# Attention of a fused perceiver layer: nine of 17 key tiles of the probabilities turned by VectorE and DMAs

## The reference, cut to what matters

```
q      = layernorm(x) @ Wq          # 32 heads of 128, in 4 groups of 8
k, v   = concat(ctx, layernorm(x)) @ Wk, @ Wv    # 2048 + 128 = 2176 keys, 4 KV heads
scores = q k^T / sqrt(128)          # 128 x 2176 per head
attn   = softmax(scores)
x      = x + (attn @ v) @ Wo
```

## Time and profile before

| | us |
|---|---|
| median of three runs | 699.45 (698.38 to 700.05) |
| the profiled execution | 698.99 |
| its span in the trace | 697.3 |
| TensorE busy | 671.9 (96%) |
| VectorE, ScalarE, GpSimd busy | 436.9, 356.7, 117.1 |
| granted TensorE clock, mean | 0.988 of full speed |

### The profile page before, as it was taken

How to read it: one execution, slowest core, us unless ns; L and a number is a source line. 1 busy time by engine, 2 the same in 40 slices (tenths; PEclk the granted TensorE clock), 3 DMA queues, 4 the chain that set the end, 5 groups by cost and what they waited for, 6 DMA issues and landing times.

```text
span 697.3 us, 12695 instructions
## 1 busy us (share of the span) xinstructions
PE 671.9 (96%) x4450; PEld 575.4 (83%) x4450; DVE 436.9 (63%) x1095; ACT 356.7 (51%) x706; POOL 117.1 (17%) x75
## 2 busy tenths in 40 slices
PE   7999998999999999999999987997999999999897
PEld 6888887899999999999999977996797797796453
DVE  2533115767777777677677765779857757756562
ACT  4403116667776677678766652664435435434101
POOL 0000001112431143114321133022220220200100
PEclk9999999999999999999999999998999999999989
DMA  8511001011021110311031503953577667647702
GB/s 257 240 61 60 1 1 61 1 56 67 1 71 52 64 56 0 120 60 60 0 111 50 240 12 145 293 199 144 203 242 264 223 238 274 214 175 276 283 20 98
DMA packets 15701, 87.07 MB, mean 125 GB/s; under 512 B 3584, under 2 KB 3968, under 8 KB 6064
## 3 DMA queue, kind: packets, MB, share of 16 engines
q1 hardware_dynamic: 15088, 85.52, 34.0%
q10 hardware_dynamic: 576, 1.05, 0.5%
HBM read 86.30 MB, written 0.26 MB: 124 GB/s over the span
## 4 chain that ended last, share of the span: by engine, by line
PE 92%; DVE 4%; ACT 2%; DMA 1%; issue 1%; SPq 0%; DVEq 0%; ACTq 0%
PE ps L1284 18%; PE ps L1079 15%; PE ps L1080 15%; PE ps L1081 14%; PE ps L1191 8%; PE ps L1324 8%; PE ps L1148 4%; PE ps L1313 2%; PE ps L1396 2%; PE ps L1431 2%; DMA ring<-wk_dram 1%; PE ps L1295 1%; PE ps L1304 1%; PE ps L1296 1%; DVE acc L922 1%; ACT prob L524 1%
## 5 line engine op out<-in xcount | busy, mean ns | idle before, releaser
L711 DVE TENSOR_TENSOR pt_lo<-ps,pt_hi 128x512 fp32r<-128x512 f32 x144 | 95.1, 661 | 72.0 <-ACT pt_hi L442 71.1
L1284 PEld LDWEIGHTS ps<-norm_t,ring 128*128 128x128 f32 x1152 | 132.6, 193 | 4.8 <-issue 3.9
L1284 PE MATMUL ps<-norm_t,ring 128*128 128x128 f32 x1152 | 133.8, 276 | 0.0
L442 ACT ACTIVATE pt_hi<-ps 128x512 fp32r<-128x512 f32 x144 | 82.2, 571 | 85.0 <-PE ps L1191 84.7
L524 ACT ACTIVATE prob<-prob,neg_max 128x512 f32<-128x512 f32 (+1 forms) x128 | 94.6, 741 | 7.5 <-DVE neg_max L803 7.5
L922 DVE SCALAR_TENSOR_TENSOR acc<-raw,cw,acc 128x127 f32<-128x127 f32 (+2 forms) x240 | 78.5, 402 | 27.9 <-ACT acc L622 27.9
L799 DVE TENSOR_SCALAR_CACHE_REDUCE prob<-ps 128x512 f32<-128x512 f32 (+1 forms) x160 | 92.0, 605 | 2.6 <-PE ps L1081 1.2
L1079 PE MATMUL ps<-pt_hi,v_hi 128*128 128x256 f32 x272 | 88.3, 325 | 0.0
L1191 PE MATMUL ps<-ident,prob 128*128 128x128 f32 x544 | 83.2, 273 | 1.9 <-DVE pt_lo L711 1.3
L1191 PEld LDWEIGHTS ps<-ident,prob 128*128 128x128 f32 x544 | 65.2, 140 | 14.9 <-DVE pt_lo L711 2.2
L1080 PE MATMUL ps<-pt_hi,v_lo 128*128 128x256 f32 x272 | 76.4, 281 | 0.0
(11 more groups left out here) (170 smaller groups left out, 1097.6 us busy)
## 6 DMA issues: line engine op xcount, KB each, us to landing
ring<-w_in_dram SPq DMA_DIRECT2D x36, 1024.0 KB, 4.8
ring<-w_out_dram SPq DMA_DIRECT2D x16, 1024.0 KB, 4.8
ring<-wq_dram SPq DMA_DIRECT2D x8, 1024.0 KB, 5.9
ring<-wo_dram SPq DMA_DIRECT2D x8, 1024.0 KB, 4.8
ring<-w_dram SPq DMA_DIRECT2D x4, 896.0 KB, 6.0
ring<-ctx_t_dram SPq DMA_DIRECT2D x3, 1024.0 KB, 6.8
ring<-w_dram SPq DMA_DIRECT2D x3, 1024.0 KB, 4.7
ring<-wk_dram SPq DMA_DIRECT2D x4, 256.0 KB, 8.2
```

The source lines that it names most:

```text
L442: copy = lambda dst, src: nc.scalar.activation(dst, src, ACT.Copy)
L711: sub = lambda dst, a, hi: nc.vector.tensor_tensor(dst, a, hi, ALU.subtract)
L1284: ins = mm(ps[:, bank, t * T:t * T + T], w[:, t, c, :], norm_t[:, c, :], start=(c == 0), stop=(c == NC - 1))
```

## The change

Pairs 0 to 14 are worked differently. Units 0 to 3 (eight key tiles, "near", 1024 keys) stay as they were. Units 4 to 8 (nine tiles, "far", 1152 keys) are no longer transposed by TensorE: VectorE transposes each head's far part in 32x32 blocks within its partitions (`turn_far`), 16 DMAs a pair carry the blocks to their place (`moves`: from 32 partitions to 32 partitions, 2304 bytes each), ScalarE takes `pt_hi` from there, and GpSimd, not VectorE, computes `pt_lo` of these units (`far_split`). The last pair is all on TensorE as before. `prob` becomes two near buffers and one far buffer.

The first four score chunks of a pair are computed two pairs ahead, in units 6, 7 and 8 (`AHEAD_AT`), the other six in units 0 to 2 (`SCORES_AT`). Queries move from unit 5 to 3, the output product from units 6 and 7 to 4 and 5, the output weights' high part from unit 2 to 0. Exps begin with the far pieces. At the start the second pair's queries stand ahead of the first scores, its first four chunks behind them, and the third pair's queries go into pair 0. On SP the weight loads are put between the moves.

```diff
-EXP_AT = ((), (), ((0, 0),), ((0, 1), (0, 2)), ((0, 3),), ((1, 0), (1, 1)), ((1, 2),), ((1, 3),), ())
-K_AT = {2: {5: (0,), 6: (1,), 7: (2,), 8: (3,)}, 3: {0: (4,)}}
+EXP_AT = ((), ((0, 2), (0, 3)), ((0, 0), (0, 1)), ((1, 2), (1, 3)), ((1, 0),), ((1, 1),), (), (), ())
+PE_UNITS = 4
+NEAR = 4 * PE_UNITS * P // 2
+FAR = KV_LEN - NEAR
+FAR_T = FAR // P
+MOVES = 16
+SCORES_AT = ((4, 5), (6, 7), (8, 9), (), (), (), (), (), ())
+AHEAD_AT = ((), (), (), (), (), (), (0,), (1,), (2, 3))
+K_AT = {2: {2: (0,), 3: (1,), 4: (2,), 5: (3, 4)}}
-W_UNIT = 2
-OUT_UNITS = (6, 7)
-Q_UNIT = 5
+W_UNIT = 0
+OUT_UNITS = (4, 5)
+Q_UNIT = 3
...
@@ SP
+            def moves(m):
+                sp.wait_ge(turned, 2 * m + 2)
+                if m >= 2:
+                    sp.wait_ge(pfl_ok, FAR_UNITS * (m - 1))
+                for i in range(4):
+                    for j in range(4):
+                        sp.dma_start(far_t[m % 2][32 * j:32 * j + 32, i, :, :, :],
+                                     blocks_t[32 * i:32 * i + 32, j, :, :, :]).then_inc(moved, 16)
+            moves(0)
+            load(2, wq[2], 2)
+            for n in range(LAST_PAIR - 1):
+                kv, p = n // PAIRS, n % PAIRS
+                if p == 2:
+                    load(0, wo[2 * kv + 2], 3 + kv)
+                if p == 0 and kv:
+                    load(1, wo[2 * kv + 1], 2 + kv)
+                moves(n + 1)
+                if p == 1 and kv < KVH - 1:
+                    load(3, wq[2 * kv + 3], 2 + kv)
+                if p == 3 and kv < KVH - 2:
+                    load(2, wq[2 * kv + 4], 3 + kv)
...
@@ GpSimd
+            def far_split(n, u):
+                w = 2 if u < 8 else 1
+                pool.wait_ge(pth_ok, UNITS * n + u + 1)
+                sub(unit_of(pt_lo[u % 3], w), far_unit(n % 2, u, w),
+                    unit_of(pt_hi[u % 3], w).bitcast(F32)).then_inc(pfl_ok, 1)
...
+                for u in range(PE_UNITS, UNITS):
+                    if n < LAST_PAIR:
+                        far_split(n, u)
+                    if more and p == 2 and u > PE_UNITS:
+                        k_split(kv + 1, u - PE_UNITS - 1)
+                    if more and p == 3 and u == 6:
+                        v_split(kv + 1, 0)
...
@@ ScalarE
+                if u < PE_UNITS or near_only:
+                    act.wait_ge(t_ps, PE_UNITS * n + u + 1)
...
+                else:
+                    act.wait_ge(moved, 16 * MOVES * (n + 1))
+                    copy(unit_of(pt_hi[u % 3], w), far_unit(b, u, w)).then_inc(pth_ok, 1)
...
@@ VectorE
+            def turn_far(m, h):
+                dve.wait_ge(exp_ok, 2 * NPC * m + (2, 6)[h])
+                if h == 0 and not (isinstance(m, int) and m == 0):
+                    dve.wait_ge(moved, 16 * MOVES * m)
+                nc.vector.transpose(blocks_t[:, :, :, h, :].rearrange("p j t q -> p t j q"),
+                                    far[:, h, :].rearrange("p (t j k) -> p t j k", j=4, k=32)).then_inc(turned, 1)
...
+                    if u in (2, 3) and not (last and p >= 2):
+                        turn_far(n + 1, u - 2)
...
@@ VectorE, start
+            q_split(1, 1, 6)
             for c in range(1, 10):
                 scores_out(0, 0, c)
...
+            turn_far(0, 0)
+            scores_out(1, 1, 0)
+            scores_out(1, 1, 1)
+            turn_far(0, 1)
+            scores_out(1, 1, 2)
+            scores_out(1, 1, 3)
+            pt_split(0, 0)
+            pt_split(0, 1)
```

More of the change, by code:

```diff
@@ L262, in out_chunk, with prob, far_unit, unit_of @@
             return step_chunk(g, 4 + i)
+        def prob(b, h, lo, hi):
+            return near[b][:, h, lo:hi] if lo < NEAR else far[:, h, lo - NEAR:hi - NEAR]
+        def far_unit(b, u, w):
+            at = 2 * (2 * u - 2 * PE_UNITS)
+            return far_t[b][:].rearrange("p i t h q -> p i (t h) q")[:, :, at:at + 2 * w, :]
+        def unit_of(tile, w):
+            return tile[:, 0:w, :].rearrange("p w (h i q) -> p i (w h) q", h=2, i=4)
         block = ctx.enter_context(nc.Block())
@@ L550, in attn_step @@
                     tgt = u + 2
-                    if tgt < UNITS or not (last and turn):
+                    if u == 2 and not (last and turn):
+                        for h, i in EXP_AT[u]:
+                            soft_exp(n + 1, 1 - b, h, i)
+                    if tgt < UNITS:
                         act.wait_ge(pv_ps, 9 * n + u + 1)
-                        pt_split(9 * n + tgt, tgt % UNITS, 4 + (9 * p + tgt) % 2)
+                        pt_split(n, b, tgt, last and turn)
+                    elif not (last and turn):
+                        act.wait_ge(pv_ps, 9 * n + u + 1)
+                        pt_split(n + 1, 1 - b, tgt - UNITS, False)
                     if u == 0 and not first:
@@ L560, in attn_step @@
                         wo_split(kv, p)
-                    if not (last and turn):
+                    if u != 2 and not (last and turn):
                         for h, i in EXP_AT[u]:
                             soft_exp(n + 1, 1 - b, h, i)
-                    if u == Q_UNIT + 1 and not first and not (last and p >= 2):
+                    if u == Q_UNIT + 1 and not (last and p >= 2):
                         q_split(n + 2, b, 6 + (1 - b))
@@ L1209, in attn_step @@
                     tgt = u + 2
[L1210 to L1217, removed]
+                    if tgt < PE_UNITS or (last and turn and tgt < UNITS):
+                        pe.wait_ge(ptl_ok, PE_UNITS * n + tgt - 1)
+                        transposes(n, b, tgt)
+                    elif tgt >= UNITS and not (last and turn):
+                        pe.wait_ge(ptl_ok, PE_UNITS * n + 2 + tgt - UNITS + 1)
+                        transposes(n + 1, 1 - b, tgt - UNITS)
                     if u == 0:
@@ L1222, in attn_step @@
                             pe.wait_ge(ql_ok, n + 2)
[L1223 to L1226, removed]
+                    values(n, b, u, kv if p == 0 else None, last and turn)
+                    if not (last and turn):
+                        for c in SCORES_AT[u]:
+                            if turn and c == 4:
                                 pe.wait_ge(kl_ok, NCHUNK * (kv + 1) + c + 1)
@@ L1242, in _ @@
             queries(0, 0, 0, 7)
+            queries(1, 0, 1, 6)
             pe.wait_ge(k_ev, 17)
@@ L1249, in _ @@
                 scores(0, 0, c)
-            queries(1, 0, 1, 6)
-            pe.wait_ge(ql_ok, 1)
-            queries(2, 0, 2, 7)
             queries_done(1, 1)
-            pe.wait_ge(exp_ok, NPC + 1)
-            transposes(0, 0, 0, 0, 4)
-            transposes(0, 1, 0, 1, 5)
+            pe.wait_ge(ql_ok, 2)
+            for c in range(4):
+                scores(1, 1, c)
+            transposes(0, 0, 0)
+            transposes(0, 0, 1)
             attn_step(0, 0, True, False)
```

106 lines of the change are left out of this document (57 added, 49 removed).

## The result

The changed kernel takes 686.20 us (median of four runs, 685.27 to 687.21), the kernel before 698.96 beside it (four runs): 12.8 us less, ratio 0.9819 [0.9802, 0.9835]. The forecast was 678.0 in a range of 672 to 704. So the sign and the range held, and 8 us of the gain that was forecast did not come. Medians of one kernel differ by up to 1.6 us from one set of runs to the next (the kernel before took 698.96, 699.37, 699.31 and 700.55), and one execution of the variant warm, 1321.84 us, is left out together with its trace. The profiled execution took 687.21 us with a span of 685.5; before it was 698.99 with 697.3, so the two spans differ by 11.8 us, against the 21.4 of the sum.

The account below looks back on a forecast made before the run. TensorE was taken to bound the kernel. Start +1.65, pairs 1 to 13 -25.7, late GpSimd +7.4, pair 14 -1.98 - 2.8: total -21.4 from 698.99, giving 677.6, with 0.46 for the median 678; range 672 to 704 us.

Parts of the forecast that it names:

- rival (a): A part is late (ScalarE copies, GpSimd at 1.5 to 1.8 us, or a common port): still faster, 684 to 698; chance 0.21.
- The bound and the gross gain: In attention, time is what TensorE issues; 18 transposes fewer a pair save 1.98 us, 29.7 us over 15 pairs.
- Durations taken from other rows: Times of new instructions, from nearest profile rows: VectorE turn 1.36 us, GpSimd far subtraction 1.29 and 0.75, ScalarE copy 0.62.
- rival (c): GpSimd's far subtraction in pieces of 32 is slow: gain gone at 1.83 us, total 709 at 2.0; chance 0.09.
- Late GpSimd in third and fourth pairs: GpSimd's K and V splits delay far groups: 1.7 us in third pairs, 0.75 in fourth, 7.4 us together.
- The form of (a) with a shared port: VectorE's turns and GpSimd's subtractions exclude each other in the loop: 1.3 us a pair, total 697; chance 0.06.
- D: Time from VectorE's turned far part to its blocks moved by SP's DMAs: 9.2 us, ends 7.5 and 15.6.
- the cover of 3.8: In a plain pair the moves are done at 19.5 us and ScalarE asks at 23.3: 3.8 us to spare.
- Rival (b): DMA round trip becomes the bound, its cycle of 4.1 us plus turned-to-moved time passing 17.1: 715 at 15.6; chance 0.11.
- The start: Up to pair 1: later first subtraction, first moves and far groups make pair 1 start 1.65 us later, 139.35 against 137.7.
- Pair 14: The last pair but one saves 1.98 us of transposes and 2.8 us of score chunks done earlier.
- The last pair: All on TensorE, it takes as long as before: 0 us.

Follow-up runs that it names:

- warm: Changed kernel plus 20 dummy matmuls in TensorE's stop ahead of pair 0's first far value products: 686.61 us, ratio 0.9819.
- small: Changed kernel with GpSimd's K and V low parts of KV heads 1 to 3 cut to almost nothing (products wrong): 679.9 us, one run.
- vord: Changed kernel with GpSimd's first V low part in fourth pairs put behind all far subtractions instead of ahead of group 7: 682.32 us, ratio 0.9742.
- lock: Changed kernel with GpSimd's first three V low parts waiting at the start until VectorE has done its last K low part: 684.68 us, ratio 0.9787.
- m32: Changed kernel with each move cut in two, the same bytes in 32 DMAs a pair: 815.4 us, one run.
- warm3: Changed kernel, GpSimd's first V low parts waiting for VectorE's last K low part, TensorE's two start stops filled with 10 and 17 small products: 683.16 us, ratio 0.9760.
- first: Changed kernel with pair 0 all transposed by TensorE, so that the first moves through SyncE are pair 1's: 681.78 us, ratio 0.9750.
- warm2: Changed kernel, GpSimd's first V low parts waiting for VectorE's last K low part, 14 and 36 dummy matmuls in TensorE's two start stops: 686.95 us, ratio 0.9814.
- best: Changed kernel with pair 0 on TensorE, GpSimd's first V parts after VectorE's last K part, fourth pairs' first V part behind far subtractions: 677.26 us, ratio 0.9679.
- dvelo: Changed kernel with the far low parts computed on VectorE instead of GpSimd: 696.6 us, one run.

## Why the prediction came out as it did

- **The range: held partly by its width.** 686.2 is outside the forecast's own 672 to 684 and in the band that the prediction gave to rival (a), 684 to 698. But (a)'s causes, slow ScalarE copies, slow GpSimd subtractions or stretched turns, are not what the traces show, so (a) was not right either.
- **The bound and the gross gain: right.** TensorE's periods fell by 1.93 us in a plain pair (1.98 forecast), and nothing but TensorE limited a plain pair.
- **Durations taken from other rows: right.** Turn 1378 for 1.36, GpSimd's far part 1290 for 1.29, 739 for 0.75, ScalarE's copy 618 for 0.62. So the short pieces of 32 cost GpSimd nothing that shows, and rival (c) is out.
- **Late GpSimd in third and fourth pairs: right.** 1.42 and 1.01 us late, forecast 1.7 and 0.75; small and vord show the cause.
- **The form of (a) with a shared port: out for the turn, true elsewhere.** 28 of the 30 turns ran beside a subtraction of GpSimd, and neither they (1369 to 1381 ns, all 30) nor GpSimd's far parts (1262 to 1312 ns) are stretched. The exclusion hit a subtraction with two SBUF inputs that fell beside GpSimd's first V part (lock), which costs 1.65 us at the second turn.
- **The DMAs: the term that was mis-sized.** "D = 15 x 0.48 + 2.0 = 9.2": landing 2.1 is right, the spacing is 0.635 and not 0.48, and some issues take 1.6 to 2.1. D is mostly 11.5 in the loop (12.0 and 12.6 in its last two pairs) and 12.7 at the start. The upper neighbour, 0.62, was in the working and put down to the crowd of weight loads; it was the nearer one. In the loop that cost nothing, as the cover of 3.8 shrank to about 1.4 and no pair used it up. At the start it cost 3.5 us: 2.3 by the spacing, 1.1 by the one long issue, 0.1 by the landing. Rival (b) was not far: the bound lies at 13.0 by the prediction's own cycle of 4.1 + D, and m32, at 26.2 for 26.4, bears that cycle out.
- **The start: forecast +1.65, measured +8.3.** 1.9 is the second turn's lateness (lock takes 1.65 of it away), 3.5 the longer D. From the first far products the forecast left 7.97 us to the start of pair 1 (131.4, which is 129.3 and the 2.1 from landing to products, to 139.35), and it took 9.06: 1.1 more. warm3 shows 8.09 with the clock whole, which puts the clock's share at 0.97. The last 0.2 is a reading: pair 1 began at 137.52 before, not at 137.7. By first, sending pair 0 through the round trip at all was a loss of 4.3 us.
- **Pair 14: 1.5 us worse than forecast.** TensorE stops once for 1.00 us in pair 14, ahead of 384.68, behind ScalarE's exps (ScalarE works without a break from 379.23 to the far copies at 382.66) and GpSimd's far part. Pair 14 takes 14.00 to 14.08 us in the traces of lock, vord, small, warm2, warm3, first and best too, so this is no chance. The prediction subtracted 2.8 us of work there and didn't ask who is late once TensorE is that much quicker. No run tested this.
- **The last pair: 1.1 us that isn't the change.** From its start to the state-space block, in windows of the kernel before, the changed kernel and small, whose code there is the changed kernel's:
```profile
403.31:422.73 19.42, 13.52 (x96) 11.52 (x94) 11.49 (x24) 9.04 (x16) 8.44 (x11) 1.00 0.17 55
```
```profile
390.39:410.89 20.50, 14.74 (x94) 12.27 (x94) 10.76 (x22) 8.90 (x16) 8.44 (x11) 0.84 0.60 241
```
```profile
384.19:403.63 19.44, 13.54 (x94) 11.62 (x93) 10.77 (x22) 8.91 (x16) 8.43 (x11) 1.00 0.60 248
```
With the clock at 1.00 it takes what it took before, as forecast (warm2 and warm3: 19.46 each). At 0.84 it takes 1.1 us more, with the last output products 0.43 us apart for 0.23; lock (0.90) and vord (0.82) have it too, 20.57 and 20.92. What makes the clock fall in one execution and not in another stays open. It moves whole times: of the 24 executions of the kernel before beside the experiments, the 15 with a mean granted clock of 0.985 or more took 698.1 to 699.5 us, the 9 at 0.983 or less 700.0 to 701.0. So a difference of 1 to 2 us between two kernels is better read from the same stretch of both traces than from their medians.

## What to carry to other kernels

A move of many small DMAs is priced by their number on the issuing queue (here 0.6 us each, with 72 KB as with half of that): work out the round trip from it, and keep it off the places where nothing can stand beside it, which are the first and the last step of a pipeline. When work is taken off the bounding engine, walk the other engines' queues in each kind of step; it is the rare step with extra work, not the plain one, that shows the new bound. And before filling a stop, ask how long the engine would have waited anyway.

## What the runs showed of the hardware that was not expected

- A DMA from SBUF to SBUF over 32 partitions holds SyncE for 591 ns and the next starts 0.635 us after it, with 72 KB as with 40 or 32 KB; in most traces a few of the 240 take 1.6 to 2.1 us. It lands 2.1 us after its issue, once 3.9 (best).
- VectorE's subtraction of two SBUF tiles of 128 x 128 took 1.94 us beside a GpSimd subtraction and 0.29 without it; in dvelo those of 128 x 512 took 906 to 1926 ns beside one and 647 to 694 without. VectorE's 32x32 block transposes of 1152 elements (1378 ns) and GpSimd's work beside them left each other alone.
- A stop of 2.2 us was followed by a granted clock of 0.81 over the next 9 us, and one of 4.3 us by 0.80 over 8.4; filled with small products, the clock stayed at 1.00. But the stop alone doesn't decide it: TensorE stands for 2.0 us near 123 in six traces, and behind that the clock fell to half for 3.4 us in the changed kernel, small and vord, and stayed at 1.00 in lock, m32 and dvelo.
- The same 3.4 us at half clock cost 0.97 us in the changed kernel and 0.33 in lock, where they fell on products for which GpSimd set the pace.
- A small product in float32 takes 0.22 us on TensorE, a transpose of the same shape 0.11.
